# Key sums in one multiply-and-sum operation on VectorE: two attention layers and a feed-forward block on one core

## The reference

```
x = x + alpha * softmax((x Wq)(ctx Wk)^T / sqrt(512)) (ctx Wv) Wo        # L0, one head
for i in (1, 2):                                                          # L1
    h = layer_norm(x, scale_i, offset_i)
    q = h wq_i + bq_i;  k = ctx wk_i + bk_i;  v = ctx wv_i + bv_i         # 16 heads of 128
    k, v get one more row: bias_k_i, bias_v_i
    x = x + softmax(q k^T / sqrt(128)) v wo_i + bo_i
h = layer_norm(x, scale, offset)
x = x + gelu(h w_fc1 + b_fc1) w_fc2 + b_fc2
```

## Time and profile before

| | |
|---|---|
| median of three runs | 1840.83 us |
| the profiled execution | 1845.13 us |
| its span | 1843.3 us |
| TensorE busy | 1814.3 us, 98% |
| VectorE busy | 1119.8 us, 61% |
| ScalarE busy | 806.2 us, 44% |
| GpSimd busy | 773.3 us, 42% |

### The profile page before, as it was taken

The page is one execution under the profiler, slowest core; times in us unless marked ns, Lnnn a source line. Parts: engine busy times, 40 slices in busy tenths (PEclk is TensorE's granted clock), DMA queues, the critical chain, the costliest instruction groups (busy, mean ns, idle before and its releaser), DMA issues.

```text
span 1843.3 us, 30698 instructions
## 1 busy us (share of the span) xinstructions
PE 1814.3 (98%) x11548; PEld 1777.6 (96%) x11548; DVE 1119.8 (61%) x2518; ACT 806.2 (44%) x1868; POOL 773.3 (42%) x634
## 2 busy tenths in 40 slices
PE   8889999999999999999999999999999999999999
PEld 5789999999999999999999999999999999999999
DVE  3676556555575565566688555556666566555565
ACT  3534344434444434344475443444435334434354
POOL 2685252453162352531378245343245252353244
PEclk9999999999999999999999999999999999999999
DMA  8952011111020121210372112121112021111132
GB/s 249 241 172 63 29 53 41 47 58 41 12 76 24 47 59 34 64 31 29 109 227 85 39 47 58 30 58 41 30 52 59 24 62 31 47 58 41 35 100 85
DMA packets 73590, 123.80 MB, mean 67 GB/s; under 512 B 13888, under 2 KB 25536, under 8 KB 73444
## 3 DMA queue, kind: packets, MB, share of 16 engines
q1 hardware_dynamic: 71140, 117.64, 21.8%
q10 hardware_dynamic: 2304, 4.20, 0.7%
HBM read 119.20 MB, written 2.61 MB: 66 GB/s over the span
## 4 chain that ended last, share of the span: by engine, by line
PE 89%; DVE 5%; DMA 2%; ACT 2%; SPq 1%; issue 1%; DVEq 0%; ACTq 0%
PE psum L589 27%; PE psum L590 27%; PE psum L591 27%; PE psum L875 4%; DMA ctxT_in<-ctxT_dram 1%; DVE xT L1536 1%; DMA ctx_rows_in<-ctx_dram 1%; PE psum L750 1%; PE psum L841 1%; DVE h_lo L1342 1%; PE psum L602 1%; PE psum L598 1%; DVE psum L1504 1%; PE psum L599 0%; PE psum L768 0%
## 5 line engine op out<-in xcount | busy, mean ns | idle before, releaser
L471 POOL TENSOR_TENSOR wbuf_hi<-stage,zero_col 128x512 fp32r<-128x512 f32 x256 | 267.5, 1045 | 916.1 <-PE psum L591 545.2
L521 POOL TENSOR_TENSOR wbuf_lo<-stage,wbuf_hi 128x512 fp32r<-128x512 f32 x256 | 329.5, 1287 | 20.1
L589 PE MATMUL psum<-pT_hi,ctx_rows_hi 121*128 121x250 f32 (+3 forms) x1152 | 332.0, 288 | 1.2 <-DVE pT_lo L1338 1.2
L591 PE MATMUL psum<-pT_hi,ctx_rows_lo 121*128 121x250 f32 (+3 forms) x1152 | 332.3, 288 | 0.0
L590 PE MATMUL psum<-pT_lo,ctx_rows_hi 121*128 121x250 f32 (+3 forms) x1152 | 331.1, 287 | 0.0
L589 PE MATMUL psum<-ctxT_hi,a_hi 128*125 128x362 f32 (+1 forms) x832 | 280.5, 337 | 0.0
L1338 DVE TENSOR_TENSOR a_lo<-psum,a_hi 128x500 fp32r<-128x500 f32 (+2 forms) x288 | 146.2, 526 | 210.2 <-ACT a_hi L996 209.5
L591 PE MATMUL psum<-ctxT_hi,a_lo 128*125 128x362 f32 (+1 forms) x832 | 273.2, 328 | 0.0
L590 PE MATMUL psum<-ctxT_lo,a_hi 128*125 128x362 f32 (+1 forms) x832 | 272.9, 328 | 0.0
L589 PE MATMUL psum<-a_hi,wbuf_hi 128*128 128x400 f32 x720 | 254.0, 353 | 0.0
L590 PE MATMUL psum<-a_lo,wbuf_hi 128*128 128x400 f32 x720 | 248.4, 345 | 0.0
(11 more groups left out here) (183 smaller groups left out, 3563.8 us busy)
## 6 DMA issues: line engine op xcount, KB each, us to landing
stage<-head_w_dram SPq DMA_DIRECT2D x256, 256.0 KB, 2.6
mlp_stage<-mlp_w_dram SPq DMA_DIRECT2D x32, 512.0 KB, 3.9
ctx_rows_in<-ctx_dram SPq DMA_DIRECT2D x12, 726.0 KB
ctxT_in<-ctxT_dram SPq DMA_DIRECT2D x12, 724.0 KB, 10.3
key_stage<-head_w_dram SPq DMA_DIRECT2D x32, 256.0 KB, 7.4
l0w<-l_w_dram ACTq DMA_DIRECT2D x16, 256.0 KB, 8.4
kb<-diff_scratch SPq DMA_DIRECT2D x32, 64.0 KB, 4.3
out_dram<-y_out SPq DMA_DIRECT2D x8, 200.0 KB, 2.6
```

Source lines behind the costliest of these rows:

```text
L471: return nc.gpsimd.tensor_tensor(out, in_, zero_col[0:in_.shape[0], :].broadcast_to(tuple(in_.shape)), ALU.add)
L521: nc.gpsimd.tensor_tensor(lo, held, hi.bitcast(F32), ALU.subtract).then_inc(stage_free, 1)
L589: pe.matmul(out, a_h, x_hi, start=start, stop=False)
L591: return pe.matmul(out, a_l, x_hi, start=False, stop=stop)
```

## The change

1. GpSimd's products and VectorE's sums of a head become four `tensor_tensor_reduce` operations on VectorE, each multiplying 128x128 by 128x128 and adding up along the row. Each is issued as two instructions, the operation and one that writes out the sum. The `kw` buffers are gone.
2. 25 heads are still done before the first layer's attention: 20 in the ramp, none in the middle of the normalisation (four stood there), and five behind it (two stood there). The other seven are done one by one in steps (0,1) to (1,3) of the first layer, from one pair of late buffers that SP fills between the weight loads.
3. `key_parts(0)` moves into the middle of the normalisation, `key_parts(1)` from step (0,0) to step (3,2).
4. GpSimd makes all eight `ctx_rows_lo` without products between them, and then splits the weights of the first two pieces at once. The third piece waits for 21 key sums, the fourth (with the clearing in front of it) for 25, where it waited for 32.
5. The first four `kb` and `key_stage` buffers now lie where the `dv` buffers lay. So SP waits for the two writes out of those (`dv_out`) and issues the first four heads' loads before any of the second turn's contexts. A load of a later head waits for the sum seven heads before it, not for the product.

```diff
-KEYS = 7
+KEYS, EARLY_KEYS, KEY_WBUF = 7, 4, 2
+LATE_KEYS_AT = {(0, 1): 1, (0, 2): 1, (0, 3): 1, (1, 0): 1, (1, 1): 1, (1, 2): 1, (1, 3): 1}
+LATE_KEYS_BEHIND = {8: 1, 14: 1, 15: 3, 17: 1, 21: 1}
+LATE_KEYS = sum(LATE_KEYS_AT.values())
+KEYS_BEFORE = LAYERS * H - LATE_KEYS
...
             sp.wait_ge(diff_out, 16)
+            sp.wait_ge(dv_out, 32)
+            some_key_weights(EARLY_KEYS)
             for b in range(3):
                 sp.wait_ge(ls_mm, b + 1)
-                if b == 0:
-                    some_key_weights(4)
                 load_ctx_columns(1, b)
...
-            some_key_weights(LAYERS * H - 11)
-            pool.wait_ge(kw_s, LAYERS * H)
+            for b in range(NB):
+                ctx_rows_lo(0, b)
+            for b in range(NB):
+                ctx_rows_lo(1, b)
...
+                        if ph == 0 and i == KEY_WBUF:
+                            pool.wait_ge(kw_sum, max(k for k in range(KEYS_BEFORE) if k % KEYS >= EARLY_KEYS) + 1)
                         if ph == 0 and i == WBUFS - 1:
-                            pool.wait_ge(kw_sum, LAYERS * H)
+                            pool.wait_ge(kw_sum, KEYS_BEFORE)
...
             def key_sums(i):
-                dve.wait_ge(kw_s, i + 1)
-                nc.vector.tensor_reduce(w0[:, :, i], kw[i % len(kw)][:, :, :], AX_X, ALU.add).then_inc(kw_sum, 1)
+                if i < KEYS_BEFORE:
+                    dve.wait_ge(kb_ld[i % KEYS], i // KEYS * 32 + 32)
+                    held, diffs = key_stage[i % KEYS], kb[i % KEYS]
+                else:
+                    dve.wait_ge(late_ld, (i - KEYS_BEFORE) * 32 + 32)
+                    held, diffs = key_stage_late, kb_late
+                for c in range(DC):
+                    summed = nc.vector.tensor_tensor_reduce(
+                        out=chunk(held, c), in0=chunk(held, c), in1=diffs[:, :], scale=1.0, scalar=0.0, op0=ALU.mult,
+                        op1=ALU.add, accum_out=w0[:, c, i:i + 1])
+                summed.then_inc(kw_sum, 1)
...
                 if j == 0:
-                    some_key_sums(4)
+                    key_parts(0)
...
                 if ph == 0:
-                    some_key_sums(LAYERS * H - 30)
+                    some_key_sums(KEYS_BEFORE - 20)
...
-                        if ph == 0 and before is None:
-                            key_parts(1)
...
+                    if ph == 0:
+                        some_key_sums(LATE_KEYS_AT.get((k, b), 0))
+                        if (k, b) == (3, 2):
+                            key_parts(1)
```

More of the change, by code:

```diff
@@ L182, in build @@
                 prob0 = sb("prob0", [P, 2, T], F32, batches)
-                kb = [sb(f"kb{j}", [P, P], F32, batches) for j in range(3)]
+                kb = [sb(f"kb{j}", [P, P], F32, batches) for j in range(EARLY_KEYS, KEYS)]
             sb("l0w_space", [P, 4 * DC * D], F32, single)
@@ L192, in build @@
                 dv_hi, dv_lo = split("dv", [LAYERS * H, P], bias_rows)
-            kw = [sb(f"kw{j}", [P, DC, P], F32, single) for j in range(2)]
-            kb += [sb(f"kb{j}", [P, P], F32, single) for j in range(3, KEYS)]
-            kw += [sb(f"kw{j}", [P, DC, P], F32, single) for j in range(2, 4)]
+            kb_first = [sb(f"kb{j}", [P, P], F32, single) for j in range(EARLY_KEYS)]
+            key_stage = [sb(f"key_stage{j}", [P, D], F32, single) for j in range(EARLY_KEYS)]
         with ExitStack() as mlp:
@@ L215, in build @@
         dv3 = sb("dv3", [65, 2, 2 * P], F32R)
+        with ExitStack() as before_aside:
+            key_stage_late = sb("key_stage_late", [P, D], F32, before_aside)
+            kb_late = sb("kb_late", [P, P], F32, before_aside)
         aside_hi, aside_lo = split("aside", [P, N])
         with ExitStack() as before_layers:
-            key_stage = sb("key_stage", [P, KEYS, D], F32, before_layers)
+            sb("first_wbufs", [P, KEY_WBUF * 2 * D], F32, before_layers)
+            key_stage += [sb(f"key_stage{j}", [P, D], F32, before_layers) for j in range(EARLY_KEYS, KEYS)]
+        kb = kb_first + kb
         w_hi, w_lo = zip(*[split(f"wbuf{j}", [P, D]) for j in range(WBUFS)])
@@ L438, in _ @@
                         load_weights(ph, i)
+                        if ph == 0:
+                            some_key_weights(LATE_KEYS_BEHIND.get(i, 0))
                         if ORDER[i][0] == "v" and ORDER[i][1] % 2 == 0:
@@ L521, in split_weights @@
                 nc.gpsimd.tensor_tensor(lo, held, hi.bitcast(F32), ALU.subtract).then_inc(stage_free, 1)
-            keys = iter(range(LAYERS * H))
-            def some_key_weights(count):
-                for _ in range(count):
-                    key_weights(next(keys))
             key_diff()
-            ctx_rows_lo(0, 0)
-            ctx_rows_lo(0, 1)
-            ctx_rows_lo(0, 2)
-            some_key_weights(3)
-            ctx_rows_lo(0, 3)
-            some_key_weights(3)
-            ctx_rows_lo(1, 0)
-            some_key_weights(2)
-            ctx_rows_lo(1, 1)
-            some_key_weights(1)
-            ctx_rows_lo(1, 2)
-            some_key_weights(2)
-            ctx_rows_lo(1, 3)
-            some_key_weights(LAYERS * H - 11)
-            pool.wait_ge(kw_s, LAYERS * H)
+            for b in range(NB):
+                ctx_rows_lo(0, b)
+            for b in range(NB):
+                ctx_rows_lo(1, b)
             for half in range(HALVES):
@@ L1171, in queries_hi @@
                 def queries_hi(h):
+                    if ph == 0 and h == ASIDE[0]:
+                        act.wait_ge(kw_sum, LAYERS * H)
                     nc.scalar.activation(made_queries(h)[0], made("q", h), ACT.Identity, bias=bias_of(BQ, h))\
```

43 lines of the change are left out of this document (21 added, 22 removed).

## The result

The changed kernel takes 1851.01 us (median of 6 runs, 1844.58 to 1854.37), the kernel before 1839.75 us (1837.81 to 1841.92): ratio 1.0056, 95% interval 1.0043 to 1.0068. It is slower, by 10.3 us by the ratio and 11.3 us by the medians; forecast were 4.8 us. The two profiled executions stand 7.4 us apart (1852.57 and 1845.13 us), and that is the difference the traces can account for.

A forecast was written before the change was run, and what follows sets the result against it. TensorE, busy nearly all the time, was taken as the bound, with only the first 170 us able to gain. Terms 1 + 3.5 - 2 + 2 + 0.3 = +4.8 us on 1840.8 gave 1845.6 us; 8-in-10 range 1835 to 1853 us.

The forecast's parts named there:

- The price of a head: VectorE's four new operations, each with its small write: 1.3 us a head, bounds 0.9 and 2.3, 0.7 us more than now.
- D: Rival, chance 0.11: the new operation runs at half rate, 2.0 to 2.3 us a head; +11 us, 1852 us.
- Rival B: Chance 0.28: early weights win at the normalisation, with heads at about 1.0 us or less; about -4.5 us, 1836.3 us.
- (b): Ramp: heads 4 and 5 delay `h_lo`, one operation held by GpSimd's `ctx_rows_lo`; +3.5 us, bounds 0 and 9.
- (c): Normalisation: ends earlier, five heads behind it delay clearing and q2, `key_parts(1)` wait goes; -2 us, bounds -6 and +3.
- (a): SP's queue in the ramp: waiting for `dv` writes delays heads and contexts 8 us, mostly hidden; +1 us, bounds 0 and 4.
- (e): First layer: seven late heads fit VectorE's idle time, `key_parts(1)` goes where it hides; +0.3 us, bounds 0 and 2.
- (d): Ramp and first layer's start: TensorE's new pauses bring stretches at half clock; +2 us, bounds 0 and 6.
- A: The forecast itself, chance 0.40: operations held in the ramp; +1 to +10 us, around +4.8.

The follow-up runs named there:

- operation alone: Kernel before with only VectorE's multiply-and-sum replacing GpSimd's products and VectorE's sums, first weight splits behind the last sum: 1853.56 us, ratio 1.0076.
- three edits: Changed kernel with turn 1's contexts loaded ahead of SP's wait, GpSimd's turn-1 row residuals in thirds, three more heads before the normalisation: 1840.22 us, ratio 0.9999.
- thin late heads: Kernel with the three edits, the seven late heads summed over 16 of 128 columns (results not the reference's): 1838.82 us, ratio 0.9989.
- three, no late heads: Kernel with the three edits, late heads undone, all 32 heads summed before or in the normalisation: 1849.97 us, ratio 1.0058.

## Why the prediction was right in sign and short in size

**The price of a head** (1.3 us, bounds 0.9 to 2.3): below the lower bound; 0.85 us. D is refuted. 128 columns from two SBUF sources with an accumulator take 0.28 us, 0.21 us apart, and per column that is no slower than the four of 200 columns without one (1.43 us). So the Trainium skill's rule on halved throughput, which the prediction cites beside D, is not seen in this operation; whether the page means this operation, CUSTOM_DVE_ANT_0 in the trace, no run shows. Rival B said that the price decides from about 1.0 us a head on down, and the prediction called itself wrong if the pair took 0.25 us or less; it took 0.21, and neither B nor C came. The price was not what decided. With 0.85 us a head the forecast's own terms come to about +2 us: (b) loses the 0.9 us by which two heads are cheaper, and in (c) the clearing comes 1.2 us later in place of 3.5, within the cover, so that the 2 us for q2 go. That the change was clearly slower all the same is in part luck: terms that were too small made up for a price that was too high.

Two sums among the rivals do not come out. B's terms, with (a) and (e) as forecast and nothing for (b) and (d), give 1 - 3.9 + 0.3 = -2.6 us, not -4.5. D's twenty heads at 2.0 us are 14 us more than in A, not 20.

**(a), +1 us**: too small, and its premise is what failed. SP resumed at 51.33 us, not 54.9, yet ScalarE waited 5.31 us. I counted the queue as full until then either way. It was not: with SP waiting, the share of the DMA engines was 0.01 from 50 to 52 us, where it was 1.02 before. With the contexts ahead of the wait it is 0.99 (326 GB/s), and that gives 3.5 us, although it exposes (b).

**(b), +3.5 us**: the mechanism is right, the heads are others. Heads 4 and 5 went free because (a) made GpSimd's rows late (84.63 us); heads 6 and 7 were held for 3.63 and 3.60 us, which stood in the upper bound only.

**(c), -2 us**: about right as a sum, -1.5 us in the two profiles, but not by the wait that it named. Its first parts are right: both `h_lo` take 1.43 us, and from the instruction behind the subtractions to the end of the second `h_lo` there are 9.1 us (131.06 to 140.21) where there were 12.9 (125.43 to 138.37), the 3.8 us of the forecast. The clearing comes 15.4 us behind the last `cen` (17.7 expected, 14.2 before). From the last `cen` to the first `prob` it is 31.5 us, where it was 30.0 (155.4 less 125.43): +1.5 us, where the forecast had +2 for q2. TensorE stands only 0.53 us for q2's split, though, and 3.99 us for `a_lo`. Behind the first `prob` the forecast had -3.9 us, and -3.0 came: the wait of 2.21 us is 0.86 us, and the slow stretch behind it (0.57; 1.7 us) is gone:

```profile
169.01 0.55 PE L872 MATMUL psum<-ident,prob 125*121 125x125 f32 x3 [0.86 <-DVE pT_lo L1337]
```

```profile
170.00:180.00 10.00, 10.00 (x72) 10.00 (x71) 6.40 (x15) 5.21 (x14) 3.04 (x3) 1.00 0.20 63
```

That `key_parts(1)` made that wait is not shown: in the kernel with the operation alone it stands at its old place, and TensorE waits 0.38 us. And of the 30.0 us ahead of the first `prob` some 3 went to the half clock in this execution of before, so a usual one may be shorter there. From the last `cen` to the first `prob` the kernel with the three edits takes 26.2 us (123.81 to 150.0), so the gain that B saw ahead of the attention is real and the five heads took it. They were priced by what they did to GpSimd's clearing; their other effect, that TensorE stands 3.99 us for `a_lo` and then runs at 0.59 (147 to 153 us), stands in (d) only, with 2 us for all places together.

**(d), +2 us**: about right for the clock itself, 1.3 us in the profiles up to the first `prob` and some 3 us by the clocks of all runs. What was too small is the pauses before the slow stretches.

**(e), +0.3 us**: too small. The 1574 us from the first `prob` to the last are the same only because the 3.0 us that (c) gained there are lost again, more than the upper bound of 2. Where TensorE stands for it is seen in part: 1.38 us at the last late head, one of whose operations was held (1.36 us at 242.07), so that `xT` behind it came late; there is no such wait before:

```profile
246.82 0.45 PE L586 MATMUL psum<-a_hi,wbuf_hi 128*128 128x400 f32 x1 [1.38 <-DVE xT L1544]
```

The run with thin late heads puts them at 1.5 us in the profiles and 1.8 by the ratios, with overlapping intervals. The two kernels without late heads take 1571.3 (operation alone) and 1573.2 us (three, no late heads) from the first `prob` to the last, where the changed one takes 1574.3. The rest stays open. This wait lies at 247 us, outside the 170 us to which the prediction looked. Nor did nearly all of TensorE's pauses lie in those before the change: 17.3 of 29.0 us did.

In the traces the ramp carries 5.6 us (last `cen` 131.06 against 125.43), the first layer's start 1.5 us, and behind it -3.0 and +3.2 cancel. The forecast for the ramp, (a), (b) and a part of (d), was 4.5 to 6.5 us, and (c) came to -1.5; so what is short in the profiles is (e), by 2.9 us. The other 3 to 4 us between 10.3 by the ratio or 11.3 by the medians and the profiles' 7.4 are what makes the profiled execution of before long; no trace of a shorter one shows where they lie.

"Taking the products off GpSimd itself gives nothing" was true, and hid the larger point that the run with the operation alone shows: the products were GpSimd's way to be done early. Without the early splits and the late heads, the same operation costs 13.9 us. Its moves won back only 2.6 us of that (by the medians; the intervals overlap), since their side effects, the three pauses, cost the 10.5 us that the edits took away. The profile of the kernel with the three edits reaches the attention 5.4 us earlier than that of before, while their medians agree. That is no riddle: 5.4 us is also what the profiled execution of before lies above its median. If the rest of the program takes as long as in the profile, a usual execution of before reaches the attention at about 150 us as well (an estimate, from the medians). By the clocks of all runs the mended kernel even loses some 2 us less to the clock than before (0.9991 against 0.9978) and spends them elsewhere: each mended kernel still has three or four pauses of 1.1 to 2.4 us between 60 us and the attention, at other places in each.

## What to carry to other kernels

When work moves from one engine to another, look first at what the old engine did next and what now releases it: here a wait for the last product became one for the last sum, and TensorE stood 12.34 us for it. Price an operation with two SBUF inputs on VectorE by what GpSimd runs beside it (3.6 us beside one of 3.5), not by its own 0.28 us. Before you call a delay in a queue hidden, look whether the queue has other work in that time. And set two profiles against each other only with the clock and the median of their kernels at hand: here the one of before was 5.4 us too long.

## What the runs showed of the hardware

- The multiply-and-sum of 128x128 in fp32 with both sources in SBUF takes 0.28 us, 0.21 us from start to start; reading the accumulator (0.08 us) is hidden.
- A copy with one SBUF source (CAST 128x64, 0.18 us elsewhere) took 2.47 us and ended with GpSimd's second clearing, which reads nothing. The earlier trace rows has another copy of 1.29 us. So for this copy neither one source nor a neighbour that only writes was a protection; the prediction had called the form with one input immune, from the reduction of the earlier trace rows, which was never held.
- Three operations in place of GpSimd's one of 3.5 us took 3.8 to 4.0 us for three of the four contexts, and 5.2 us for the first; the longest hold of VectorE fell from 3.63 to 1.38 us.
- Executions of one kernel differ with the granted clock: of 86 of the kernel before, those at 0.996 took 1844.1 us in the mean, at 0.997 1842.6, at 0.998 1840.1 and at 0.999 1839.8.
